# The denominators of the second attention, in odd steps, moved behind the scores and beside the first value products

## The reference, cut to what matters

```
kv_input = jnp.concatenate([x, lat], axis=1)
k = (kv_input @ Wk)...;  v = (kv_input @ Wv)...;  q = (lat @ Wq)... * SCALE
sim = jnp.einsum('bhqd,bhfd->bhqf', q, k)
sim = sim - jax.lax.stop_gradient(jnp.max(sim, axis=-1, keepdims=True))
sim = jnp.where(kv_mask, sim, -jnp.inf)
alphas = jax.nn.softmax(sim, axis=-1)
out = jnp.einsum('bhqf,bhfd->bhqd', alphas, v)
return out.transpose(0, 2, 1, 3).reshape(b, q_len, INNER) @ Wo
```

## Time and profile before

| | |
|---|---|
| median of three runs | 3412.47 us |
| profiled execution, its own time | 3420.25 us |
| its span | 3418.6 us |
| busy over the span | PE 92%, PEld 67%, DVE 65%, POOL 48%, ACT 39% |
| second attention, about 948 to 2780 us | PE 1798.4 of 1832 us |
| `d_rb` reciprocals, L2156 | 256, mean 920 ns |
| POOL additions, L2235 | 448, mean 2.4 us |

### The profile page before, as it was taken

The page is one execution under the profiler, slowest core; times in us unless marked ns, Lnnn a source line. Parts: engine busy times, 40 slices in busy tenths (PEclk is TensorE's granted clock), DMA queues, the critical chain, the costliest instruction groups (busy, mean ns, idle before and its releaser), DMA issues. The chain is left out here.

```text
span 3418.6 us, 58879 instructions
## 1 busy us (share of the span) xinstructions
PE 3139.7 (92%) x18273; PEld 2301.0 (67%) x18274; DVE 2215.2 (65%) x5164; ACT 1342.4 (39%) x2056; POOL 1652.5 (48%) x981
## 2 busy tenths in 40 slices
PE   4885999999889999999999999999999975879978
PEld 4655888888756666666666666666666663679966
DVE  5667455555657777777777777777786654235545
ACT  2332333333334444444444444444444441234422
POOL 5002333333246656565566565666666644770047
PEclk7995999999989999999999999999999967989999
DMA  4000000001111111212112121111120032342253
GB/s 113 1 0 1 19 14 14 9 14 58 74 57 63 62 62 37 84 42 82 43 57 79 45 73 45 62 65 59 41 77 35 7 109 82 131 150 72 72 178 104
DMA packets 118348, 204.62 MB, mean 60 GB/s; under 512 B 13792, under 2 KB 85544, under 8 KB 112432
## 3 DMA queue, kind: packets, MB, share of 16 engines
q1 hardware_dynamic: 105200, 173.30, 15.0%
q0 software_dynamic: 12992, 29.72, 2.9%
HBM read 141.28 MB, written 61.64 MB: 59 GB/s over the span
## 5 line engine op out<-in xcount | busy, mean ns | idle before, releaser
L2235 POOL TENSOR_TENSOR d_acc<-d_acc,d_pr 128x1024 f32<-128x1024 f32 x384 | 937.1, 2440 | 90.4 <-ACT d_pr L2089 59.9
L2089 ACT ACTIVATE d_pr<-d_p 128x1024 f32<-128x1024 f32 x512 | 487.0, 1027 | 241.4 <-PE d_p L2016 241.4
L1949 PE MATMUL d_pO<-d_pr,d_V 128*64 128x512 f32 x2048 | 473.0, 599 | 0.0
L2235 POOL TENSOR_TENSOR d_acc<-d_pr 128x1024 f32<-128x1024 f32 x64 | 153.3, 2396 | 626.0 <-ACT d_pr L2089 626.0
L2145 DVE TENSOR_REDUCE d_nm<-d_p 128x2 f32<-128x1024 f32 x256 | 303.7, 1220 | 87.4 <-PE d_p L1992 87.4
L938 POOL TENSOR_TENSOR e_hs<-e_hf,e_hs 128x512 fp32r<-128x512 f32 x136 | 175.7, 1292 | 365.2 <-ACT e_hs L913 365.2
L2140 DVE CUSTOM_DVE_ANT_0 d_biased<-d_p,d_masked 128x512 f32<-128x512 f32 x512 | 330.5, 687 | 27.9 <-issue 27.9
L1949 PEld LDWEIGHTS d_pO<-d_pr,d_V 128*64 128x64 f32 x2048 | 135.4, 136 | 261.5 <-issue 235.0
L968 DVE SCALAR_TENSOR_TENSOR res<-e_pY,m_Wt,res 128x256 f32<-128x256 f32 x544 | 225.8, 477 | 44.7 <-PE e_pY L874 43.9
L2156 DVE RECIPROCAL d_rb<-d_rb 128x128 f32<-128x128 f32 x256 | 224.6, 920 | 8.4 <-ACT d_rb L2082 8.4
L959 DVE TENSOR_TENSOR e_hf<-e_sl,e_pU 128x512 f32<-128x512 f32 x136 | 93.5, 688 | 209.0 <-ACT e_sl L910 209.0
(11 more groups left out here) (323 smaller groups left out, 5870.9 us busy)
## 6 DMA issues: line engine op xcount, KB each, us to landing
d_W<-w_split SPq DMA_DIRECT2D x30, 1536.0 KB, 6.9
d_masked<-mask_bias SPq DMA_DIRECT2D x64, 256.0 KB
kv_split<-d_parts SPq DMA_DIRECT2D x56, 256.0 KB, 5.6
d_kv<-kv_split SPq DMA_DIRECT2D x7, 2048.0 KB, 11.2
x_slots<-m_zeros SPq DMA_DIRECT2D x1, 9088.0 KB, 28.6
b_x<-x_slots SPq DMA_DIRECT2D x71, 128.0 KB, 2.0
y_slots<-b_y SPq DMA_DIRECT2D x71, 128.0 KB, 1.7
xh_split<-m_XH SPq DMA_DIRECT2D x8, 1024.0 KB
```

Source lines behind the costliest of these rows:

```text
L1949: last = pe.matmul(pO[own[h], :], V[vb][:, s, par * P + h * HD1:par * P + (h + 1) * HD1], pr[:, s % PT, h, :], start=(s == 0), stop=(s == ...
L2089: act.activation(pr[:, n % PT, :, :], slot(st, what, n)[:, :, :], ACT.Exp).then_inc(exp_done, 1)
L2235: pool.tensor_tensor(acc[:, q, :, :], a, pr[:, s % PT, :, :], ALU.add).then_inc(acc_done, 1)
```

## The change

In the list of odd steps, `den` moves from behind `VV0` to behind `S2`, which itself stands behind `ST7`; `r0` to `r3` move from among `ST6`, `ST7` and `S2` to among the value products: `r0 r1` behind `PV1`, `r2 r3` behind `PV3`. Nothing is added or removed; the list of even steps is as it was.

```diff
-    """Q X KK M VV0 den S0 ST0 ST1 S1 ST2 ST3 ST4 ST5 ST6 r0 ST7 r1 r2 S2 r3 PV0 PV1 PV2 PV3 S3 S4 S5 PV4 PV5 PV6 PV7
+    """Q X KK M VV0 S0 ST0 ST1 S1 ST2 ST3 ST4 ST5 ST6 ST7 S2 den PV0 PV1 r0 r1 PV2 PV3 r2 r3 S3 S4 S5 PV4 PV5 PV6 PV7
        S6 S7 T VV1 N Z O YY""".split())
```

## The result

The changed kernel takes 3471.8 us (median of 5 runs, 3466.2 to 3475.1), the one before 3412.5; the ratio is 1.0169, 95% interval [1.0158, 1.0181], and the growth 59.3 us. Predicted were 3462 us, a growth of 50, in a range of 3432 to 3474.

What follows compares the result with a forecast made beforehand. PE bounds the second attention, so only its start times count; 15 x 1.7 + 7 x 1.5 + 6 x 2.6 - 1.3 = +50.3 us on the median 3412.5 gives 3462 us, range 3432 to 3474.

Steps and rivals of the forecast that it cites:

- Front of the step: Odd step's start on PE: denominators cost 0.91 us, ST1 waits for ACT's copy, POOL's first addition comes 0.90 us earlier.
- Denominators, copy, four reciprocals: Chain behind S2 in odd steps: denominators at 1517.88, ACT's copy until 1519.60, four reciprocals 3.42 us, normalisation at 1523.05.
- The meeting with POOL: DVE's normalisation starts 0.09 us behind POOL's fifth addition, loses the shared ports, and ends 0.55 us after that addition.
- loop-first step: First odd step of a batch-loop pass: race lost by 0.2 us, VV1 2.6 us later; six steps, 15.6 us.
- ordinary step: The common odd step: race newly lost, S3 to S5 late on DVE, VV1 1.7 us later; fifteen steps, 25.5 us.
- special one: Odd step whose normalisation already lost to POOL before the change: loses again, 1.5 us later; seven steps, 10.5 us.
- The last batch: Its four odd steps: POOL's additions follow more slowly, so no lost race, 0.1 us less each; with the tail -1.3 us.
- Half of the races lost: First rival: ordinary steps win their race, the thirteen others lose; +23 us, 3436 us; chance 0.13.
- none lost: Second rival: reciprocals or copy some 0.2 us earlier, or POOL later, so no race lost; +2 us, 3414 us; chance 0.10.
- faster: Third rival: PE gains at the odd step's front, ST0's wait and the tail; -8 us, 3404 us; chance 0.04.
- Worse through N: Fourth rival: late DVE passes through N to the next step's M, another 1.5 us in 28 steps; 3504 us; chance 0.05.
- The filler term: Denominators filled PE's wait for d_KL ahead of ST0; moved away, they cost 0.9 us in six loop passes, 5.4 us.

Runs made afterwards that it cites:

- the first experiment: The changed kernel with reciprocals and normalisation reading the PSUM bank and ACT's copy left out: 3419.5 us, ratio 1.0016 to the kernel before.
- the long fill: The changed kernel plus a 1024-element one-partition fill on POOL between its first and second addition of odd steps: 3419.7 us, ratio 1.0008 to the kernel before.
- the reciprocals alone: Against the kernel before, only the reciprocals move among the value products; denominators stay ahead of S0: 3446.4 us, ratio 1.0094.
- the short fill: The changed kernel plus a 512-element one-partition fill on POOL between its fourth and fifth addition of odd steps: 3478.4 us, ratio 1.0190 to the kernel before.
- denominators-only run: Against the kernel before, denominators move behind S2, but three reciprocals stay ahead of S2's passes on DVE and one behind: 3467.2 us, ratio 1.0142.
- X behind S1: Changed order with reciprocals and normalisation in PSUM, plus odd steps' tile preparation X moved on DVE behind S1: 3567.2 us, ratio 1.0439 to the kernel before.

## Why the prediction was right, point by point

**PE is the bound, and nothing but its start times counts.** Right: with the normalisation in PSUM, on the order of before, 38 waits of DVE are gone and the time stays (ratio 0.9994); the first experiment and the long fill, whose VV1 starts in time, lie within 0.2% of the kernel before.

**Front of the step.** The denominators' 0.91 is right, and S0 and ST0 moved as worked out. ST1 does wait for ACT's copy of V, but that does not reach POOL: ACT's second exponential starts right behind its first all the same. So POOL's first addition came 0.99 us earlier (6.68 behind VV0 for 7.67), not 0.90, and the race was lost by 0.16 instead of 0.09. That did not change who won; it made the end of the addition, and VV1 with it, 0.1 us earlier than summed.

**Denominators, copy, four reciprocals.** The normalisation was put at 1523.05 with VV0 at 1506.33, 16.72; it starts 16.70 behind VV0 (1538.82 - 1522.12). This sum out of handovers of three other steps held to 0.02 us, and not by errors that cancel: S2 was put 11.23 behind VV0 and starts at 11.22.

**The meeting with POOL.** Right, and the traces narrow where it tips. Between two additions, 0.05 to 0.08 us ahead wins (the reciprocals alone), and in a loop-first step of the kernel before so did 0.02 (1690.23 for 1690.25, 0.69 us long). In the last batch of the changed kernel the normalisation started 0.02 us behind the addition and lost:

```profile
2696.80 2.88 DVE L2160 TENSOR_TENSOR d_OT<-d_osb,d_rb 128x512 f32<-128x512 f32 x1
```
```profile
2696.78 2.36 POOL L2235 TENSOR_TENSOR d_acc<-d_acc,d_pr 128x1024 f32<-128x1024 f32 x1
```

The rule of the Trainium skill (SBUF — State Buffer, Who interferes with whom), that the first to issue has the shared ports for the whole instruction and that a DVE operation with at most one SBUF input outside the two-port modes does not contend, agrees with the changed kernel, with the PSUM version (0.69 beside 2.37) and with the waits of X. The one case against its letter is the short fill, where POOL's addition had the port before its recorded start.

**The price.** An ordinary step costs 1.6 us (1.7 predicted), a special one 1.14 to 1.53 (1.5), a loop-first one 2.2 to 3.1 (2.6). Twelve undisturbed ordinary intervals, 19.4, are 1.0 less than 12 x 1.7; the special ones 9.5 for 10.5; the loop-first ones 14.9 for 15.6. The signs named ahead came too: 2.5 to 2.8 us for the normalisation in all but one odd step up to 2583 us (1.88 in the one with the lowered clock), and 0.91 for the denominators. PE's wait for `d_KL` in the six loop-first steps was 0.9 to 1.6 us long, not 1.7.

**The last batch: wrong.** The prediction reckoned no lost race there, 0.1 less for each of four. Two intervals grew by 1.85 and 1.89 us, and the third odd step lost its race as well; only the last won. POOL's slower pace was right: its fifth addition starts 10.12 us behind its first there (2696.78 - 2686.66), 9.86 in the ordinary step. What failed is that I concluded the race from the pace alone, without adding up its start. The first addition comes 0.16 us earlier there (6.52 behind VV0, 6.68 in the ordinary step), which leaves 0.10 of those 0.26, and with a normalisation 0.04 earlier that brings the margin from 0.16 to 0.02, and not below nothing. The normalisation was ahead by 0.31 before chiefly because it came 0.25 earlier behind VV0 (14.80 for 15.05), and behind the four reciprocals hardly any of that is left (16.66 for 16.70). That is close to 6 us missing from the sum.

**The clock: not in the sum.** The trace of the changed kernel has four stretches of 3.4 us at half the TensorE clock inside the second attention, starting at 1238, 1603, 2009 and 2299 us; that of the kernel before has none between 976 and 2737 us. The second, with VV1 in it, which starts at 1602.54 (columns as in rows 1):

```profile
1602.00:1604.00 2.00, 1.74 (x11) 1.50 (x11) 2.00 (x3) 1.21 (x3) 1.64 (x1) 0.78 0.00 0
1604.00:1606.00 2.00, 2.00 (x11) 2.00 (x11) 1.25 (x3) 0.00 (x0) 0.00 (x0) 0.50 0.00 0
1606.00:1608.00 2.00, 2.00 (x13) 1.89 (x13) 0.00 (x0) 0.78 (x1) 0.00 (x0) 0.87 0.00 0
```

Ahead of it PE had waited in the three places above; then the granted clock was 0.50, the level of 1.2 GHz, and the projection took 4.48 us to YY's start at 1607.02, instead of 2.95 to 2.98. The other two of this kind, at 2009 and 2299 us, begin 0.5 us behind VV1's start as well. The three intervals with such a drop grew by 3.1 instead of 1.6. The one at 1238 us comes behind another wait, that of ST0 for `d_KL` (1.60 us, until 1236.61), in the loop-first interval with 3.1 where the others have 2.2 to 2.5. So some 5 us of the growth go with clock drops that stand right behind PE's pauses. I had thought of worse cases only as a wait passed on, and not of this one.

So the mechanism predicted is the right one and its price for a step nearly right; that the sum came near is in part luck, since what was missed and what was too large cancel in part. From the first VV0 to the last normalisation the traces grew by 57 us: 28.7 in the fifteen ordinary intervals (25.5 predicted; some 24 without the clock drops), 9.5 in the special ones (10.5), 14.9 in the loop-first ones (15.6), 3.7 in the last batch and 0.1 behind its last VV0, where a third race lost and an end nearly 2 us earlier cancel (-1.3 for both). The 59.3 us between the medians hold some 2 more, which no trace places and which are less than the spread of the runs. The measured time is inside the range, but only 2 us from its end.

**The rivals.** Half of the races lost, none lost, and faster: excluded, 31 of 32 are lost. Worse through N: N starts 2.25 us behind VV1 instead of 2.08 and takes 0.17 us instead of 1.83 (1547.38, and 1529.88 before), since POOL is done by then, so it ends earlier than before. The filler term (a rival's, and 0.9 x 6 in the sum) is seen by itself in the first experiment, 6.9 us for six.

## What to carry to other kernels

An idle stretch of an engine is not free room for any operation: two engines that share a port are to be laid beside each other, and the question for each operation is what it reads and what the other has under way at that moment. A lost race costs the rest of the other's instruction, however small the loser is, so long instructions on the one and element-wise work with two SBUF inputs on the other go badly together. It costs time only where the critical engine then waits for the loser: the 38 lost races of the kernel before cost nothing. One input taken from PSUM ended it here and brought 3471.8 us to 3419.5. Where a gap on the critical engine was filled by work that nobody hurried for, moving that work away costs it in full (0.8 to 1.5 us in each of six intervals here, for 0.91 of denominators).

## What was not expected of the hardware

- Short waits of PE are followed by 3.4 us at half the clock, which cost 0.9 to 1.5 us with VV1's projection in them and 0.6 to 0.9 in the loop-first interval of the changed kernel. In the reciprocals-only run it happened behind each of the seven steps that were 2.4 us late (1193, 1422, 1650, 1879, 2108, 2336, 2565 us; 1.8 us of idle time recorded at S6, S7 and VV1). In the changed kernel, with 1.1 us recorded at the same places, it happened three times in 31 steps, and not once in the denominators-only run, which is as late. Behind ST0's wait for `d_KL` it happened once there (1.60 us) and once in the long-fill run (1.57, at 1456 us), but never in the first experiment, with waits of 1.51 to 1.61. The short-fill run has one behind either kind of wait (1256 and 1935 us). With X behind S1 it happened in all 28 odd steps that have an X. What decides between the shorter waits stays open.
- A one-partition fill recorded with 0.51 us delayed POOL's next addition by 0.3 us, but its claim on the port, by my estimate from the lost races (0.26 us ahead of the recorded start), by 0.1 only. Recorded starts of POOL behind such a fill are no good measure of a race.
- `d_xhat`, a subtraction and multiplication with one SBUF tensor as input and an SBUF output, also waited for POOL (2.23 us, against 0.41 with POOL idle). One tensor input in SBUF alone does not make an operation safe; the reciprocals, with one tensor input too, never waited (0.89 to 0.97 each in all runs). The Trainium skill (SBUF — State Buffer, Who interferes with whom) names `tensor_scalar`, which this is, among the operations that can enter a two-port mode; the run agrees.
